# Keys and values of the cross-attention made beneath the alignment's walk back, spilled and loaded per step

## The reference

```
x = x + tanh(g_xattn[0]) * align(ctx, layernorm(x))        # DTW: costs, then the walk back, then rows added up
x = x + tanh(g_ffn[0])   * (causal attention + mixture of experts)(layernorm(x))
x = x + tanh(g_xattn[1]) * cross(layernorm(x), ctx, ctx, mask, Wq, Wk, Wv, Wo)
x = x + tanh(g_ffn[1])   * fp4_ffn(layernorm(x))

cross:  q = split_heads(h @ Wq.T);  k = split_heads(ctx @ Wk.T);  v = split_heads(ctx @ Wv.T)    # 16 heads of 16
        scores = (q k^T) * 4;  masked places = most negative number;  softmax;  @ v;  @ Wo.T
```

## Time and profile before

| what | value |
|---|---|
| time, median of 3 runs | 2625.43 us (2622.67 to 2633.93) |
| the profiled execution's own time | 2625.44 us |
| its span, first to last instruction | 2623.7 us |
| PE busy / DVE busy / ACT busy / POOL busy | 71% / 63% / 37% / 11% of the span |
| mean granted clock of PE | 0.793 of full |
| `backtrack` | about 476 to 699 us of the span |
| cross-attention, from its first DMA to the last copy of a step | 1552 to 2291 us of the span |

### The profile page before, as it was taken

How to read it: one execution, slowest core, us unless ns; L and a number is a source line. 1 busy time by engine, 2 the same in 40 slices (tenths; PEclk the granted TensorE clock), 3 DMA queues, 4 the chain that set the end, 5 groups by cost and what they waited for, 6 DMA issues and landing times. The chain is left out here.

```text
span 2623.7 us, 39283 instructions
## 1 busy us (share of the span) xinstructions
PE 1852.2 (71%) x12876; PEld 1103.4 (42%) x12876; DVE 1653.3 (63%) x6821; ACT 983.9 (37%) x1859; POOL 283.9 (11%) x269
## 2 busy tenths in 40 slices
PE   6999810532648888733979705999999999824884
PEld 3776510102545555431655504444454444222553
DVE  5479999897658888330101145776777776356984
ACT  1355432310016666400202002566666666622331
POOL 2000000000000000022000130000000000024662
PEclk9555555555869999955989957899999999966997
DMA  4111110300010000025031123010100000010000
GB/s 163 44 64 52 58 58 29 100 0 1 21 41 9 9 9 2 1 93 187 24 134 58 38 66 122 1 57 1 57 1 1 25 1 1 1 33 0 0 1 32
DMA packets 60542, 104.94 MB, mean 40 GB/s; under 512 B 7480, under 2 KB 42738, under 8 KB 58702
## 3 DMA queue, kind: packets, MB, share of 16 engines
q1 hardware_dynamic: 42660, 72.92, 8.0%
q10 hardware_dynamic: 14640, 22.28, 2.4%
q0 software_dynamic: 3072, 7.53, 0.9%
HBM read 70.73 MB, written 32.85 MB: 39 GB/s over the span
## 5 line engine op out<-in xcount | busy, mean ns | idle before, releaser
L1078 DVE CUSTOM_DVE_ANT_0 xam_junk<-xam_s,xa_mask_q 128x512 bf16<-128x512 f32 x512 | 339.6, 688 | 170.6 <-PE xam_s L985 169.8
L1151 ACT ACTIVATE xam_exp<-xam_s 128x512 f32<-128x512 f32 x512 | 299.7, 598 | 204.1 <-PE xam_s L1019 197.1
L985 PE MATMUL xam_s<-xa_kT,xa_qT 96*128 96x512 bf16 x512 | 197.8, 389 | 12.6 <-DVE xam_max L1078 11.1
L1016 PE MATMUL xam_s<-xa_qT,xa_kT 99*128 99x512 bf16 x512 | 196.7, 384 | 13.7 <-ACT xam_exp L1151 12.9
L1019 PE MATMUL xam_s<-xa_mask_k,identb 128*128 128x512 bf16 x512 | 195.3, 381 | 0.0
L353 PE MATMUL ps_d<-xnT,ctxT 128*32 128x112 f32 (+4 forms) x3168 | 158.2, 348 | 9.8 <-ACT stage L497 8.6
L430 DVE TENSOR_TENSOR_SCAN cost<-m,cost,dist_chunk 128x33 f32<-128x33 f32 x576 | 164.1, 285 | 0.1
L1078 DVE CUSTOM_DVE_ANT_0 l0m_junk<-l0m_s,l_tri_q 128x128 bf16<-128x128 f32 (+3 forms) x256 | 118.9, 488 | 45.6 <-PE l0m_s L985 42.8
L359 PE MATMUL ps_d<-rows_j,share 4*128 4x112 f32 (+4 forms) x396 | 140.8, 457 | 0.8 <-ACT rows_j L469 0.8
L1600 PE MATMUL ex_up<-ex_xT,ex_w 128*128 128x512 f32 x256 | 122.1, 637 | 22.6 <-DVE ex_xT L1632 13.1
L1030 PE MATMUL xam_o<-xam_exp,xa_vt 128*32 128x512 f32 x1024 | 137.2, 605 | 0.0
(11 more groups left out here) (323 smaller groups left out, 3859.7 us busy)
## 6 DMA issues: line engine op xcount, KB each, us to landing
dist_chunk<-dist SPq DMA_DIRECT2D x36, 264.0 KB
ex_w<-L_ffn_W ACTq DMA_DIRECT2D x8, 1024.0 KB, 15.9
ex_w<-L_ffn_W SPq DMA_DIRECT2D x8, 1024.0 KB, 15.9
xa_mask<-mask_BxSxS_ik SPq DMA_DIRECT2D x4, 2048.0 KB, 11.2
ctx_nat<-ctx ACTq DMA_DIRECT2D x4, 1024.0 KB, 14.3
x_sb<-x SPq DMA_DIRECT2D x2, 2048.0 KB, 12.1
ctxT_d<-ctxT SPq DMA_DIRECT2D x4, 1024.0 KB, 9.0
ctx_rows<-ctx SPq DMA_DIRECT2D x1, 4096.0 KB, 15.3
```

What stands on the lines that cost most here:

```text
L985: nc.tensor.matmul(ps1[n % 2][:, 0:w], qT[0:STK, slot(g, h), qt * P:(qt + 1) * P], kT[0:STK, slot(g, h), f * 512:f * 512 + w], start=True, ...
L1016: nc.tensor.matmul(o[:, q0:512], kT[:, slot(g, h), kt * P:(kt + 1) * P], qT[:, slot(g, h), q0:512], start=True, stop=False)
L1078: nc.vector.tensor_tensor_reduce(junk[:, n % NJ, 0:w], ps1[n % 2][:, 0:w], heads.bias_q(g, qt, f), 1.0, NEG * 4, ALU.add, ALU.max, mx[:, g ...
L1151: nc.scalar.activation(ebuf[at % NE][:, q0:512], ps2[at % 2][:, q0:512], ACT.Exp).then_inc(exped, 1)
```

## The change

1. `dtw_costs` no longer spills `ctxT`.
2. In `backtrack`, each of the 33 rounds of the row loop is followed on PE and ACT by a piece of new work (`split`), which makes 16 key tiles (rounds 0 to 15; in PSUM banks 4 to 7) and then 16 value tiles (rounds 16 to 31). A key tile is transposed from the start (features by positions): two fp32 matmuls with 512 columns, a copy to bf16 by ACT, then twice PE subtracts the kept part from the bank (one bf16 matmul by minus the identity) and ACT copies the rest. A tile's three parts are thus made over three rounds, in one of three buffers (`KEEP`), and SP stores them (384 KB) to `keys_d`. A value tile is four fp32 matmuls with 256 columns and one copy, in one of two buffers, stored (512 KB) to `values_d`.
3. ACT's first copy of tile n waits for the store of tile n-3 (`keys_out`), or, of values, of tile n-2. The PSUM pairs of the row loop are two, not four.
4. SP issues four DMAs of weights ahead of the constants. `ctx` is now loaded over `above`, when the row loop is over.
5. In cross-attention the rounds `kv` and the four `turn` of the keys are gone, with what they took on DVE, ACT and POOL. Each step's keys come by six DMAs (`load_step`, one for each group of 16 partitions, 128 KB each) and its values by one (512 KB in rows of 512 bytes). Steps 0 to 3 are loaded in the first block (`load_first`), with mask and constant rows; step p from 4 on when step p-4 is over on PE.
6. The first block has no wait for the loads any more. The tanh stands in layer norm's block. `hT` stays in SBUF, and `attend_all` isn't called here.

```diff
-        ctx = sb("ctx_rows", [P, B * KT, D], F32)
+        ctx = above[:, :, :].rearrange("p r s -> p (r s)")[:, 0:2 * B * KT * D].bitcast(F32).rearrange(
+            "p (n d) -> p n d", d=D)
+        keys = sb("kv_keys", [P, KEEP, 3, 512], BF16)
+        values = sb("kv_values", [P, 2, 2, NH, VW], F32)
 ...
+                for n, (b, t, c) in enumerate(ktiles):
+                    sp.wait_ge(kv_low, n + 1)
+                    sp.dma_start(keys_d[...], keys[:, n % KEEP, :, :]).then_inc(keys_out[n % KEEP], 16)
+                for n, (b, t) in enumerate(vtiles):
+                    sp.wait_ge(kv_high, nk + n + 1)
+                    sp.dma_start(values_d[b][:, t:t + 2, :], values[...]).then_inc(values_out[n % 2], 16)
+                sp.wait_ge(posed, RB)
+                sp.wait_ge(capping, RB)
+                sp.dma_start(ctx, d["ctx_1024"]...).then_inc(ctx_in, 16)
 ...
+                def first(n):                                   # ScalarE
+                    act.wait_ge(kv_made, n + 1)
+                    bank = ps[4 + n % 4]
+                    if n < nk:
+                        if n >= KEEP:
+                            act.wait_ge(keys_out[n % KEEP], 16 * (n // KEEP))
+                        nc.scalar.copy(keys[:, n % KEEP, 0, :], bank[:, :]).then_inc(kv_high, 1)
+                    else: ...
+                def split(n):
+                    if n < nk + nv:
+                        first(n)
+                    if 1 <= n <= nk:
+                        rest(n - 1, 1, kv_less, kv_mid)
+                    if 2 <= n <= nk + 1:
+                        rest(n - 2, 2, kv_least, kv_low)
                 for r in range(RB):
-                    o = ps[r % QT * 2:r % QT * 2 + 2]
+                    o = ps[r % 2 * 2:r % 2 * 2 + 2]
                     act.wait_ge(posed, r + 1)
                     act.wait_ge(narrowed, r + 1)
                     nc.scalar.activation(near[...])
                     nc.scalar.activation(near[...]).then_inc(shaped, 1)
+                    split(r)
 ...
-    rounds_of = ((0, ("q",)), (2, ("kv", 0)), (6, ("turn", 0, 0)), (8, ("turn", 0, 1)), (10, ("kv", 1)),
-                 (13, ("turn", 1, 0)), (16, ("turn", 1, 1)), (18, ("turn", 2, 0)), (21, ("turn", 2, 1)))
-    repeats = ((3, 0), (5, 1), (13, 2))
+    rounds_of = ((0, ("q",)), (6, ("turn", 0, 0)), (8, ("turn", 0, 1)))
+    repeats = ((3, 0),)
 ...
+    def load_step(self, sp, p):
+        b, h = p // NG, slice(p % NG * HG, (p % NG + 1) * HG)
+        rows = slice(p % NG * GW, (p % NG + 1) * GW)
+        for part, slots in enumerate(K_SLOTS):
+            for x in slots:
+                sp.dma_start(self.kT[x * HD:(x + 1) * HD, h, :],
+                             self.keys_d[part, b, rows, :].rearrange("(h e) k -> e h k", e=HD)).then_inc(...)
+        sp.dma_start(self.vt[:, :, h, :]..., self.values_d[b][...]).then_inc(self.valued[p % NG], 16)
+    def load_first(self, sp, ones):
+        self.load_mask(sp, 0)
+        self.load_step(sp, 0)
+        sp.dma_start(self.kT[STK:STK + MAXR, :, :]..., ones[...]).then_inc(self.came, 16)
+        for p in range(1, NG):
+            self.load_step(sp, p)
     def load(self, sp):
+        for p in range(NG, STEPS):
+            ...
+            sp.wait_ge(self.scored2, (p - NG + 1) * n2)
+            sp.wait_ge(self.weighed, (p - NG + 1) * n2)
+            self.load_step(sp, p)
```

More of the change, by code:

```diff
@@ L27 @@
 WIDE = 112
+KEEP = 3
 WIDTHS = (48, 64, 80, 96, 112, 112)
@@ L85, in _ @@
             nc.scalar.activation(std[:, :], std[:, :], ACT.Sqrt).then_inc(std_done, 1)
+            if also is not None:
+                also(act)
 def transpose_tokens(nc, es, src, dst, ident, name, scale=None, bias=None, mul=1.0, spill=None, ready=None):
@@ L180, in dtw_block @@
                 transpose_tokens(nc, es2, xn, lambda g, h: xnT[:, h, g * 512:(g + 1) * 512], ident, "xT", mul=-2.0)
-            dtw_costs(nc, d, dist, near, above, xnT, ctxT, ctxT_d, which, norms, spread, x_sb)
-        backtrack(nc, d, near, above, spans, x_sb, ident)
+            dtw_costs(nc, d, dist, near, above, xnT, ctxT, which, norms, spread, x_sb)
+        backtrack(nc, d, near, above, spans, x_sb, ident, identb, ctxT, keys_d, values_d)
 def norm_inputs(nc, es, d, x_sb, xn, ctxT, which, rows_i, norms, norms_d, spread):
@@ L258, in _, with dtw_costs @@
                 nc.scalar.copy(rows_i[:, LEAD + c * 512:LEAD + (c + 1) * 512], ps[c][0:B, :]).then_inc(kept, 1)
-def dtw_costs(nc, d, dist, near, above, xnT, ctxT, ctxT_d, which, norms, spread, x_sb):
+def dtw_costs(nc, d, dist, near, above, xnT, ctxT, which, norms, spread, x_sb):
     with ExitStack() as es:
@@ L526, in _, with backtrack @@
                 keep(1, NCH * CH)
-def backtrack(nc, d, near, above, spans, x_sb, ident):
+def backtrack(nc, d, near, above, spans, x_sb, ident, identb, ctxT, keys_d, values_d):
     with ExitStack() as es:
@@ L595, in _ @@
                                      ap_of(spans, i * P * RB + b * PADI + LEAD, [[P, KT], [1, P]])).then_inc(taken, 16)
+                for i in range(KEEP):
+                    sp.wait_ge(keys_out[i], 16 * len(range(i, nk, KEEP)))
+                for i in range(2):
+                    sp.wait_ge(values_out[i], 16 * len(range(i, nv, 2)))
+            @block.gpsimd
+            def _(pool):
+                nc.gpsimd.memset(values[:, :, :, :, HD:HD + 1], 1.0)
+                nc.gpsimd.memset(values[:, :, :, :, HD + 1:VW], 0.0).then_inc(padded, 1)
             @block.vector
@@ new lines, in lessen, with split @@
+                def lessen(n, part, kept, less):
+                    pe.wait_ge(kept, n + 1)
+                    nc.tensor.matmul(ps[4 + n % 4][:, :], minus[:, :], keys[:, n % KEEP, part, :], start=False, stop=True,
+                                     skip_group_check=True).then_inc(less, 1)
+                def split(n):
+                    if n < nk + nv:
+                        make(n)
+                    if 1 <= n <= nk:
+                        lessen(n - 1, 0, kv_high, kv_less)
+                    if 2 <= n <= nk + 1:
+                        lessen(n - 2, 1, kv_mid, kv_least)
@@ L1792, in project @@
             return last
[L1793 to L1798 removed]
         for i in range(QT):
             for h in range(DH):
[L1801 to L1802 removed]
+                t = p // NG * QT + i
+                last = nc.tensor.matmul(bank[:, i * GW:(i + 1) * GW], self.hT[:, h, t * P:(t + 1) * P],
+                                        self.wq[:, h, g * GW:(g + 1) * GW], start=(h == 0), stop=(h == DH - 1))
         return last
```

198 lines of the change are left out of this document (126 added, 72 removed).

## The result

| kernel | median us | ratio to before, 95% interval |
|---|---|---|
| before | 2628.4 beside it, 4 runs | 1 |
| after | 2556.6 (2547.8 to 2558.8, 4 runs) | 0.9719 [0.9701, 0.9738] |

A forecast was written before the change was run, and what follows sets the result against it. PE was taken to bound the cross-attention steps, DVE the first pass and `backtrack`. Terms -84 - 6 - 23 + 29 + 15 = -69 took 2625.43 to 2556 us (chance 0.52, own range 2535 to 2578); overall range 2520 to 2615.

The forecast's parts named there:

- Steps: Cross-attention steps: two `kv` and four turns leave PE, 6.0 us less in each of fourteen steps, -84 us.
- the 95%: Cross-attention steps: share of preparation's PE time, 9.0 of 9.45 us, taken to show in the step; applied to 6.34 us removed.
- Layer norm to the first maximum: Start of cross-attention: three waits go and less work stands between `q` and the first maximum, -23 us (ends -17 and -26).
- first pass: Cross-attention's first pass, paced by DVE: two splits, two copies and about one stall go, -6 us (ends -3 and -9).
- SP's block: Ahead of layer norm: SP must issue 33 DMAs before the barrier, so layer norm starts 33 to 40 us after the first, +29.
- the price of the keys: SP's loads ahead of layer norm: 24 key DMAs into 16 partitions each, 122 KB/us, 1.05 us apiece, 25 us.
- narrow writes go at nearly full width: Case for the loads ahead of layer norm, or the queue holds more: +8 to +14 instead of +29, 2538 us, chance 0.15.
- Row loop: `backtrack`: ACT ends at 605.7, past DVE's 590.6, with key rounds of 4.7 us paced by store landing, +15 us.
- start slip: `backtrack`: four weight DMAs ahead of the constants make PE and DVE start near 482.0 instead of 480.25.
- PE stays at 1.2 GHz: Case for the row loop of `backtrack`: PE's clock stays low, 2556 + 64 = 2620 us, no change, chance 0.12.
- Slower: Case for the row loop of `backtrack`: key stores land late, the loop grows by 106 us, 2662 us, chance 0.06.
- not hidden loads: Case for the cross-attention: steps 4 to 15 each wait for their 8 us of loads, +96, 2652 us, chance 0.02.

The follow-up runs named there:

- `q` three times: Changed kernel with every `q` projection of the cross-attention computed three times into the same bank: 2613.3 us, 0.9953 of before.
- late loads: Changed kernel with the key and value loads of steps 1 to 3 issued behind layer norm instead of ahead: 2533.3 us, 0.9650 of before.
- keys early: Changed kernel with the 18 key loads of steps 1 to 3 kept ahead of layer norm, their three value loads behind it: 2542.3 us, one run.
- four tiles: Changed kernel with four key tiles instead of three in the row loop of `backtrack` (`KEEP` = 4): 2549.6 us, 0.9707 of before.
- The fillers: Changed kernel without the key and value work, plus unread matmuls per row: two fp16, one fp32 or eight fp16; 2543.8, 2546.0 and 2543.4 us.

## Why the prediction was right, and where it was not

2556 was forecast and 2556.6 measured, with the sign of every term right. But three sizes, and one reason, were off. That the number came out within 1 us is luck: the five terms together gave 4.1 us more than forecast, and 6.2 us in stages that no term names went the other way.

**Steps, -84 forecast, -78.7 measured.** The place and the mechanism hold: the step without preparation kept its 30.28 us, and PE time costs one to one (`q` three times). The step that was mis-sized is the 95%: of 6.34 us removed 5.6 showed, 88%. In the waits of the step, PE's weight loads behind `exp` rose from 71.1 to 95.4 us between the first and the fourteenth step; that preparation had filled such waits is argued from this, not tested.

**Layer norm to the first maximum, -24.8, and first pass, -4.8,** came within 2 us of the forecast and inside their ends.

**SP's block, +29 forecast, +23.8 measured, for a wrong reason.** That 33 issues and the full queue hold layer norm was right, and late loads proved it. The step that failed is the price of the keys: "24 key DMAs of 128 KB that each write only 16 partitions", and "1.05 us for each DMA, 25 us". By the landing, the measure of my sum, a key load took 0.64 to 0.69 us, 24 of them some 16. A value load, which I had at full rate (5 to 8 us for four), took 2.5 to 2.8, four of them 10 to 11. All had landed after 38.5 us, the low end of my 39 to 46, because the two errors partly cancelled. Of that 8.5 us were left behind the last issue, where I had taken 6. What each kind costs SP is another matter: 0.47 us for a key load while the queue had room, 3.8 for a value load with its 1024 small pieces. I had taken the slope from two narrow DMAs that landed one at a time; here six neighbours are in flight together, and they write different partitions. The case "narrow writes go at nearly full width" had the key loads too fast (8 to 11 us for 24) and, as the forecast did, the values.

The rule of the Trainium skill (SBUF — State Buffer, section "Door 1: The DMA port swizzle"), applied to each key load by itself, gave 1.4 us for it and +38 in all. The trace disagrees: with keys early, 18 of them were issued in 8.40 us, and 2.07 MB, nearly all of it keys, landed in the 12 us behind that, under 0.8 us for each 128 KB. That several narrow transfers share the ports between them is my reading, and no run isolates it.

**Row loop, +15 forecast, +11.4 measured.** The pace was right to name: the key rounds were begun by the store's landing, and four tiles proved it. A round was 4.2, not 4.7: my own 4.35 stood there, and I had added for a slow clock that stayed only in the first rows. The start slip was 3.0, not 1.7: the weight DMAs took 2.65 to issue, and the first constant behind them 0.62 instead of 0.35. Value rounds were 2.97, not 2.8. ACT's end at 605.03 against 605.7 hides that the block began 3.4 us later than in the trace I read. By the first pick the term was 11.0 in this execution and 7.2 to 8.3 in the six other kernels with the same loop, so its usual size is near half of the forecast.

**The clock.** The case in which PE stays at 1.2 GHz (0.12) didn't come: 1.00 in most of the loop. The Trainium skill (TensorE: Matmul & The Clock Gate, "What's actually happening") says that activity releases the throttle; the row from 500 in the earlier trace rows seemed to speak against it. The fillers show both at once: a PE whose row reads 25.00 of 25 us stays at 0.50 with the rows and a little more, and goes to 1.00 with eight wide matmuls a row. The wide fp32 columns that I named were enough, but wide fp16 ones were enough too.

**Slower, and not hidden loads:** no key store landed later than 4.0 us, and no wait of a step is put down to a load of keys or values.

## What to carry to other kernels

A barrier waits for the queue that issues, not for what lands: count what one engine must issue ahead of it, in pieces as well as bytes, and move what isn't needed next behind it (20 us here, for two moved lines). When work is laid under another engine's cover, give its stores so many buffers that one has a whole round to land before it is written again (8 us at most here), and put its loads behind those that start the cover (3 us). And a term that comes out nearly right can rest on two errors: only the runs that split it, keys from values, showed it.

## What the hardware showed that I had not expected

- A load of 512 KB in pieces of 512 B kept the issuing queue for 3.8 us, one of 128 KB in pieces of 2 KB into 16 partitions for 0.47 while the queue had room. The two landed at about the same rate, 180 to 205 KB/us.
- A granted clock of 0.50 with PE reading busy 25.00 of 25 us, window after window to 575 us, with the rows and a small filler; 1.00 with eight wide matmuls a row.
- More work by PE and ScalarE beside DVE's scan didn't slow it: picks 117.26 and 117.27 us after the block's start, without and with it.
